# Attention phase: stacked operands filled from SBUF, transpositions placed inside accumulations, and Q of two groups ahead of K

## The chip, the cores and the metric

The program runs on one core of one Trainium2 chip. Its time is device microseconds (us) of one execution; the number compared is the median over repeated executions. The kernel before takes 1622.26 us (median of 3 runs, 1620.95 to 1627.36). All five engines of the core are used: PE (TensorE, matmul), DVE (VectorE), ACT (ScalarE), POOL (GpSimd) and SP (SyncE, which here only issues DMAs).

## The reference

Eight independent batches of 512 tokens with 512 features go through two layers. Only the first attention is touched by the change; in short:

```python
h   = layernorm(x)                                   # (8, 512, 512)
q, k, v = h @ W_Q + b_Q, ctx @ W_K + b_K, ctx @ W_V + b_V   # 16 heads of 32
attn = softmax(q @ k.T / sqrt(32)) @ v               # per head
x = x + tanh(g_xattn[0]) * (attn @ W_O + b_O)
x = x + tanh(g_ffn[0])   * bitlinear_ffn(layernorm(x))       # 8-bit activations, ternary weights
x = x + tanh(g_xattn[1]) * softmax(layernorm(x) @ ctx.T) @ ctx
x = x + tanh(g_ffn[1])   * mxfp4_linear(layernorm(x))
```

## The kernel before

**Phases.** `attention_phase` computes the first attention of all eight batches (about the first 864 us of the span); `ffn_and_final_phases` does everything after it. The change is in the first phase only.

**Precision by splitting.** Every f32 operand of a projection or a score is held as a high part and a low part (HI = rounded copy, LO = the rest), and a product is three passes, HI·HI, LO·HI and HI·LO. For scores the three passes are stacked along the contraction: a head has 32 features, so `stack[:, g, Q]` holds HI, LO, HI on partitions 0 to 31, 32 to 63, 64 to 95, and `stack[:, g, K]` holds HI, HI, LO. One matmul with 96 rows then gives a score tile. Row 96 holds ones on the K side and minus the row maximum on the Q side (`mrow`), so that the 97-row matmul gives the score less its maximum.

**Groups and slots.** Four heads (J = 4) make a group g of 128 features, four groups make a batch. For each group there are 16 steps, called slots here: one `max` matmul (96 rows; DVE reduces its row maximum, L843), and one `score` matmul (97 rows; ACT takes the exponential, L724). Twelve of the 16 exponentials are added up on POOL (L938). After the slots come the matmuls with V (`pv`, L627), and the column sums (`den`, L646), for which all of POOL's sums must be done. PE also does, between slots, the work for the batch ahead: transpositions of x and ctx tiles (`t`, L550: t0 to t3 of x, t4 to t7 of ctx), the Q and K projections (`qk`, L566: 12 matmuls each, in four pieces of 3), and the V projection of the batch itself (`v`, L580: 4 tiles of 12 matmuls).

**What sets the order.** `Clock` is a table of due times in ticks; a group has 160, a slot 8. Each engine runs all steps in the order of their times (plus an offset per engine), written out without a loop. `ahead(n)` puts a step at slot n of a count that starts with group 1 of the batch before, so that the work ahead is spread over groups 1, 2, 3 of one batch; V stands in group 0. Times only set the order; the engines run as fast as their semaphores let them.

**Two PSUM banks.** t, qk and v share banks `work0` and `work1`. `Turns` hands them out in turn, and PE waits until the bank's last user was read by both ACT and DVE.

**From a projection to the stack.** ACT writes the HI part of a projection with its bias to `part[:, side, HI]`, DVE the LO part (L691, L830). `part` has one place for Q and one for K. SP then sends both parts to DRAM (`spill`, 512 KB, L456), and when they have landed issues three loads of 256 KB (`fill`, L464), each of which takes four heads from four blocks of 32 rows to 32 partitions of `stack`. A place of `part` is free again for ACT when the spill has landed. The first `max` of group g stands 19 slots before its first `score` and waits for both fills of its group. SP issues every DMA of the phase, `mrow` among them (L470), in the order of the table, and while it waits for one, those behind it wait too.

Of the kernel before, what the change touches and what calls it, by code (L numbers as in the profile page):

```python
# [151 lines left out]
class Turns:  # L152
# [4 lines left out]
    def __init__(self, banks, users, batches, read_out):  # L157
        self.banks, self.users, self.batches, self.read_out = banks, users, batches, read_out
        self.turn = {key: n for n, (_, key) in enumerate(users)}
        assert len(users) % len(banks) == 0  # L160

    def bank(self, *key):
        return self.banks[self.turn[key] % len(self.banks)]

    def wait_free(self, engine, it, *key):
        n, back = self.turn[key] - len(self.banks), 0
        while back <= 3:
            while n < 0:
                n, back = n + len(self.users), back + 1
            shift, who = self.users[n]  # L170

            if not isinstance(it, int) or 0 <= it - back + shift < self.batches:
                self.read_out(engine, it, shift - back, who)
                return
            n -= len(self.banks)


def attention_phase(nc, NB, keep0, keep1, x, ctx_in, w_q, b_q, w_k, b_k, w_v, b_v, spill, attn_t, ctx_t, ffn_w, w_o, b_o, weight, delta_w,
# [54 lines left out]
    with ExitStack() as ctx:  # L233
# [12 lines left out]
        ct = wo  # L246
        stage = sb("stage", [P, STAGE, D], F32)
# [21 lines left out]
        brow = mrow[0:3 * G, 0, :].bitcast(F32)  # L269
# [14 lines left out]
        wv_lo, bias_turned, bias_done, ln_nmean = sem("wv_lo"), sem("bias_turned"), sem("bias_done"), sem("ln_nmean")  # L284
# [22 lines left out]
        spilled = [sem("spilled_q"), sem("spilled_k")]  # L307
# [18 lines left out]
        tx_at, tc_at = (0, 1.5, 3, 4.5), (10.8, 12.3, 13.8, 15.3)  # L326
        qk_at = {(0, Q): 6, (0, K): 16.8, (1, Q): 21.4, (1, K): 26, (2, Q): 30.6, (2, K): 35.2, (3, Q): 39.8, (3, K): 44.4}
        fill_at = {(0, Q): 17, (0, K): 25, (1, Q): 32, (1, K): 37, (2, Q): 41, (2, K): 46, (3, Q): 52, (3, K): 56}
        STORE_CT = (50, 57.5)
        ck = Clock(G * PERIOD, NB)  # L330
        for i in range(T):
# [6 lines left out]
            for c in range(C):  # L338
                ck.add(round(7.4 * (i * C + c)), 2, "v", i, c)
        for n, slot_n in enumerate(STORE_CT):  # L340
            ck.add(ahead(slot_n), 9, "ctstore", n)
        for g in range(G):
            base = g * PERIOD
            for side in (Q, K):
                for c in range(C):
                    ck.add(ahead(qk_at[g, side] + 1.15 * c), 3, "qk", g, side, c)
                ck.add(ahead(qk_at[g, side] + 1.15 * (C - 1)) + at["spill"], 9, "spill", g, side)
# [41 lines left out]
        def read_out(pe, it, shift, who):  # L389
# [5 lines left out]
            elif kind == "qk":  # L395
                wait_count(pe, qk_hi, it, shift, 2 * G, 2 * n + who[2] + 1)
                wait_count(pe, qk_lo, it, shift, 2 * G, 2 * n + who[2] + 1)
# [9 lines left out]
        turns = Turns(work, users, NB, read_out)  # L407
# [4 lines left out]
        with nc.Block() as block:  # L412
            @block.sync
            def _(sp):
# [13 lines left out]
                def window(it, shift, name, args):  # L428
# [23 lines left out]
                    elif name == "spill":  # L452
                        g, side = args
                        sync_wait(sp, held, qk_lo, it, shift, 2 * G, 2 * g + side + 1)
                        sync_wait(sp, held, stacked[g][side], it, shift, 1, 0, 48)
                        sp.dma_start(spill[g, side].rearrange("h p s -> p h s"), part[:, side].bitcast(F32))\  # L456
                            .then_inc(spilled[side], 16)
                    elif name == "fill":
                        g, side = args
                        sync_wait(sp, held, spilled[side], it, shift, G, g + 1, 16)  # L460

                        sync_wait(sp, held, s_full, it, shift, G * T * J, (g - G + 1) * T * J)
                        for n, h in enumerate((HI, LO, HI) if side == Q else (HI, HI, LO)):
# [3 lines left out]
                    elif name == "mrow":  # L467
                        g, = args
                        sync_wait(sp, held, mt_done, it, shift, G, g + 1)
                        sp.dma_start(stack[96:97, g, Q].bitcast(F32), mrow[:, g % 2, :].bitcast(F32))\  # L470
                            .then_inc(mrow_put[g % 2], 16)
# [40 lines left out]
                    elif name == "boload" and b == NB - 1:  # L512
                        sp.wait_ge(spilled[Q], 16 * G * NB)
                        sp.wait_ge(spilled[K], 16 * G * NB)
# [10 lines left out]
            def _(pe):  # L525
# [3 lines left out]
                def turn_biases():  # L529
                    pe.wait_ge(bias_loaded, 48)  # L530
                    nc.tensor.transpose(den[:, 0:3 * G], brow[:], ident[0:3 * G, 0:3 * G]).then_inc(bias_turned, 1)
# [7 lines left out]
                def window(it, shift, name, args):  # L539
# [13 lines left out]
                    elif name == "qk":  # L553
                        g, side, c = args
                        if c == 0:
                            if isinstance(it, int) and it + shift == 0 and g == 0:
                                pe.wait_ge(w_hi, side + 1)
                                pe.wait_ge(w_lo, side + 1)
                                pe.wait_ge(bias_done, 1)
# [91 lines left out]
            def _(act):  # L651
                def split_weight(n):
                    act.wait_ge(w_loaded[n], 16)
                    nc.scalar.activation(w["qkv"[n]][:, :, HI, :], probs[:, n], ACT.Copy).then_inc(w_hi, 1)
# [10 lines left out]
                def put_biases():  # L665
                    act.wait_ge(bias_turned, 1)
                    nc.scalar.activation(bias[:].rearrange("p n g -> p (n g)"), den[:, 0:3 * G], ACT.Copy).then_inc(bias_done, 1)
                    act.wait_ge(bias_done, 1)

                def window(it, shift, name, args):  # L670
# [16 lines left out]
                    elif name == "qk" and args[2] == C - 1:  # L687
                        g, side, _ = args
                        wait_count(act, qk_full, it, shift, 2 * G, 2 * g + side + 1)
                        wait_count(act, spilled[side], it, shift, G, g, 16)  # L690
# [5 lines left out]
                    elif name == "norm":  # L696
# [5 lines left out]
                        if isinstance(it, int) and it + shift == 0 and i == T - 2:  # L702
                            split_weight(0)
                    elif name == "v" and args[1] == C - 1:
# [4 lines left out]
                    elif name == "mt":  # L709
# [3 lines left out]
                        nc.scalar.activation(mrow[:, g % 2, :], den[0:J * T, 0:P], ACT.Copy).then_inc(mt_done, 1)  # L713
                    elif name == "score":
# [1098 lines left out]
```

## Time and profile before

| | us |
|---|---|
| median of 3 runs | 1622.26 |
| the profiled execution | 1623.71 |
| its span, first to last instruction | 1621.9 |
| PE busy (share of the span) | 1477.0 (91%) |
| DVE busy | 1226.8 (76%) |
| ACT busy | 875.9 (54%) |
| POOL busy | 890.9 (55%) |
| mean granted TensorE clock, of full speed | 0.958 |

The span is 1.8 us shorter than the execution's own time. Busy shares are means over stages with different limits, so they say little of one stage. Of its DMA the page gives 265.32 MB in all, with 64 spills (512 KB each, median 3.5 us from issue to landing) and 192 loads into the stack (256 KB each, 6.8 us).

### The profile page before, as it was taken

How to read it: one execution, taken by the hardware profiler on the slowest of the kernel's cores; microseconds unless marked ns; L12 is line 12 of the kernel's file. 1: busy time of each engine (PE TensorE's matmuls, PEld its weight loads, DVE VectorE, ACT ScalarE, POOL GpSimd, SP SyncE). 2: the span in 40 equal slices, each digit the busy share in tenths (PEclk: the TensorE clock that was granted, in tenths of full speed). 3: DMA queues.
4: the chain of work that ended last, by engine and by line, in shares of the span. 5: the costliest groups of instructions: out<-in, count | busy, mean ns of one | idle time of the engine just before them, and what ended most of it. 6: DMA issues, size and time to landing. Idle time of an engine off the chain costs nothing. (4 is left out here: it accounts for less than half of the span.)

```text
span 1621.9 us, 24716 instructions
## 1 busy us (share of the span) xinstructions
PE 1477.0 (91%) x6993; PEld 937.9 (58%) x6993; DVE 1226.8 (76%) x2135; ACT 875.9 (54%) x1433; POOL 890.9 (55%) x1148
## 2 busy tenths in 40 slices
PE   5699999999999889899784999999999968999997
PEld 3466666556565566655532455555555447887885
DVE  4867677777868677677662788888888848999986
ACT  4156666666565556555453555555555535555552
POOL 3166676585675757656462343343333316777775
PEclk9899999999999989999878999999999989999998
DMA  6757849485694865937941344444444653556522
GB/s 201 227 163 211 258 150 273 143 249 161 185 277 128 229 190 176 289 108 226 251 115 55 95 114 109 109 116 107 107 107 109 190 146 120 167 165 203 166 86 62
DMA packets 252172, 265.32 MB, mean 164 GB/s; under 512 B 139932, under 2 KB 162984, under 8 KB 247720
## 3 DMA queue, kind: packets, MB, share of 16 engines
q1 hardware_dynamic: 252072, 264.14, 57.4%
q8 instruction: 44, 0.72, 0.2%
q14 instruction: 56, 0.46, 0.1%
HBM read 149.50 MB, written 82.87 MB: 143 GB/s over the span
## 5 line engine op out<-in xcount | busy, mean ns | idle before, releaser
L724 ACT ACTIVATE a_probs<-a_sc 128x512 f32<-128x512 f32 x512 | 300.5, 595 | 288.5 <-PE a_sc L608 284.7
L843 DVE TENSOR_REDUCE a_negmax<-a_mx 128x1 f32<-128x512 f32 x512 | 339.0, 675 | 108.1 <-PE a_mx L591 107.3
L938 POOL TENSOR_TENSOR a_acc<-a_acc,a_probs 128x512 f32<-128x512 f32 x248 | 311.6, 1285 | 11.1 <-ACT a_probs L724 9.7
L938 POOL TENSOR_TENSOR a_acc<-a_probs 128x512 f32<-128x512 f32 x124 | 156.9, 1285 | 247.9 <-ACT a_probs L724 247.0
L591 PE MATMUL a_mx<-a_stack 96*128 96x512 f32 x512 | 231.0, 451 | 40.3 <-DVE a_negmax L843 22.3
L1089 PE MATMUL bank<-wcode,b_xq 128*128 128x512 bf16 x1024 | 229.3, 383 | 11.1 <-DMA b_xq<-b_xcode 11.1
L608 PE MATMUL a_sc<-a_stack 97*128 97x512 f32 x512 | 217.7, 427 | 21.0 <-DMA a_stack<-a_mrow 19.5
L1089 PEld LDWEIGHTS bank<-wcode,b_xq 128*128 128x128 bf16 x1024 | 100.5, 98 | 135.0 <-DMA b_xq<-b_xcode 12.5
L854 DVE RECIPROCAL a_attn<-a_den 128x128 f32<-128x128 f32 x128 | 120.8, 947 | 71.1 <-PE a_den L646 58.6
L591 PEld LDWEIGHTS a_mx<-a_stack 96*128 96x128 f32 x512 | 103.1, 201 | 114.4 <-DVE a_negmax L843 55.0
L1127 ACT ACTIVATE b_sig<-bank,b_tok 128x512 f32<-128x512 f32 x128 | 87.4, 683 | 94.0 <-PE bank L1089 91.9
L608 PEld LDWEIGHTS a_sc<-a_stack 97*128 97x128 f32 x512 | 104.0, 203 | 49.5 <-DMA a_stack<-a_mrow 18.4
L566 PE MATMUL a_work<-a_xt,k_wbuf 128*128 128x512 f32 x384 | 121.5, 431 | 12.0 <-DVE a_xt L818 12.0
L1181 DVE TENSOR_TENSOR b_hid<-b_sig,bank 128x512 f32<-128x512 f32 x128 | 87.4, 685 | 50.8 <-ACT b_sig L1127 50.8
L1131 ACT ACTIVATE b_hid<-b_hid,b_htok 128x2048 f32<-128x2048 f32 x32 | 64.1, 2003 | 102.9 <-DVE b_htok L1200 102.9
L627 PE MATMUL a_pvb<-a_probs,a_v 128*32 128x512 f32 x1024 | 118.9, 603 | 0.7 <-ACT a_probs L724 0.7
L1096 PE MATMUL bank<-wcode,b_hq 128*128 128x512 bf16 x512 | 116.1, 380 | 0.0
L566 PE MATMUL a_work<-k_wo,k_wbuf 128*128 128x512 f32 x384 | 114.5, 410 | 1.5 <-DVE k_wo L818 1.5
L1078 PE MATMUL bank<-k_wo,b_apart 128*128 128x512 f32 x384 | 101.8, 415 | 14.7 <-POOL b_apart L1232 13.8
L580 PE MATMUL a_work<-k_wbuf,k_wo 128*128 128x512 f32 x384 | 113.9, 409 | 0.0
L1503 PE MATMUL bank<-c_ct,c_xt 128*128 128x512 f32 x384 | 99.0, 408 | 11.0 <-DVE c_xt L1601 8.7
L1238 POOL TENSOR_TENSOR b_nmean<-b_mv,k_minus 128x1 f32<-128x1 f32 x32 | 6.1, 189 | 172.0 <-DVE b_mv L1153 172.0
(165 smaller groups left out, 2637.0 us busy)
## 6 DMA issues: line engine op xcount, KB each, us to landing
a_stack<-spill SPq DMA_DIRECT2D x192, 256.0 KB, 6.8
spill<-k_part SPq DMA_DIRECT2D x64, 512.0 KB, 3.5
ctx_t<-k_wo SPq DMA_DIRECT2D x16, 1024.0 KB, 9.8
c_ct<-ctx_t SPq DMA_DIRECT2D x8, 2048.0 KB, 7.9
a_stage<-in_x_dram SPq DMA_DIRECT2D x32, 256.0 KB, 5.1
a_stage<-in_ctx_dram SPq DMA_DIRECT2D x32, 256.0 KB, 3.1
a_wsum<-in_L_ffn_w_gate_dram SPq DMA_DIRECT2D x8, 1024.0 KB, 6.1
attn_t<-a_attn SPq DMA_DIRECT2D x32, 256.0 KB, 4.6
```

Of the source, the lines that this page charges most:

```text
L566: last = nc.tensor.matmul(turns.bank("qk", g, side)[:], w["qk"[side]][:, c, a, g * P:(g + 1) * P], src[:, c, m, :], start=c == 0 and n == ...
L580: last = nc.tensor.matmul(turns.bank("v", i)[:], ct[:, c, a, i * P:(i + 1) * P], w["v"][:, c, m, :], start=c == 0 and n == 0, stop=c == C ...
L591: nc.tensor.matmul(mx[i % 2][:], stack[0:96, g, Q, j, t * P:(t + 1) * P], stack[0:96, g, K, j, :], start=True, stop=True).then_inc(mx_full, 1)
L608: nc.tensor.matmul(sc[i % 2][:], stack[0:97, g, K, j, k * P:(k + 1) * P], stack[0:97, g, Q, j, :], start=True, stop=True).then_inc(s_full, 1)
L627: last = nc.tensor.matmul(pvb[DH * j:DH * (j + 1), :], v[:, k, h * DH:(h + 1) * DH], probs[:, k, j, :], start=k == 0, stop=k == T - 1)
L724: nc.scalar.activation(probs[:, k, j, :], sc[i % 2][:], ACT.Exp, scale=SCALE).then_inc(exp_done, 1)
L843: nc.vector.tensor_reduce(negmax[:, g % 2, j, t:t + 1], mx[i % 2][:], axis=AX.X, op=ALU.max, negate=True).then_inc(mx_done, 1)
L854: nc.vector.reciprocal(attn[:, g % 2, q * P:(q + 1) * P], den[:, q * P:(q + 1) * P]).then_inc(recip_done, 1)
L938: nc.gpsimd.tensor_tensor(acc[:, j], probs[:, 0, j] if k == 1 else acc[:, j], probs[:, k, j], ALU.add)\
L1078: last = nc.tensor.matmul(bank_o[:], apart[:, t % 2, a, c, :], wo[:, c, m, :], start=c == 0 and n == 0, stop=c == C - 1 and n == 2)
L1089: last = nc.tensor.matmul(bank[:], xq[:, t % 2, c, :], gu_code[:, side * M + m, :, c, :], start=c == 0, stop=c == C - 1)
L1096: last = nc.tensor.matmul(bank_d[:], hq[:, t % 2, r, :], wcode[:, 2 * M:3 * M, r, :], start=r == 0, stop=r == R - 1)
```

## The change

1. The spill to DRAM is gone. The columns of W_Q, W_K and their biases are permuted within a group when the weights are split (`permuted`, and a second transposed bias row `bpart`), so that partition 4r + j of a projection is feature r of head j. The three fills then read `part` in SBUF, in row order, and write the stack. A place of `part` is free for ACT when the three fills that read it have landed.
2. `mrow` is issued by ACT's DMA queue, not by SP's.
3. The table: transpositions of x move from group 1 into group 0 among the V accumulations; those of ctx move forward into the Q accumulations of groups 0 and 1; Q of group 1 comes before K of group 0. `BANK` names each user's bank, so that a transposition inside an accumulation has the other bank.

```diff
+        def permuted(n, h):
+            to = w["qkv"[n]][:, :, h, :]
+            src = probs[:, n].rearrange("p a b -> p (a b)").rearrange("p (c e) -> p c e", c=C)
+            if n == 2:
+                return to, src
+            return (to.rearrange("p c (g r j) -> p c g r j", g=G, j=J), src.rearrange("p c (g j r) -> p c g r j", g=G, j=J))
...
-        tx_at, tc_at = (0, 1.5, 3, 4.5), (10.8, 12.3, 13.8, 15.3)
-        qk_at = {(0, Q): 6, (0, K): 16.8, (1, Q): 21.4, (1, K): 26, ...
+        tx_at, tc_at = (-14.5, -10.7, -7.2, -3.7), (2, 7, 9.7, 11.2)
+        v_at = [3.6 * i + 0.9 * c for i in range(T) for c in range(C)]
+        ORDER = ((0, Q), (1, Q), (0, K), (1, K), (2, Q), (2, K), (3, Q), (3, K))
+        RANK = {key: n for n, key in enumerate(ORDER)}
...
-                    elif name == "spill":
-                        g, side = args
-                        sync_wait(sp, held, qk_lo, it, shift, 2 * G, 2 * g + side + 1)
-                        sync_wait(sp, held, stacked[g][side], it, shift, 1, 0, 48)
-                        sp.dma_start(spill[g, side].rearrange("h p s -> p h s"), part[:, side].bitcast(F32))\
-                            .then_inc(spilled[side], 16)
                     elif name == "fill":
                         g, side = args
-                        sync_wait(sp, held, spilled[side], it, shift, G, g + 1, 16)
+                        sync_wait(sp, held, qk_lo, it, shift, 2 * G, RANK[g, side] + 1)
                         sync_wait(sp, held, s_full, it, shift, G * T * J, (g - G + 1) * T * J)
                         for n, h in enumerate((HI, LO, HI) if side == Q else (HI, HI, LO)):
-                            sp.dma_start(stack[DH * n:DH * (n + 1), g, side].bitcast(F32),
-                                         spill[g, side, h].rearrange("(j r) s -> r j s", j=J))\
+                            sp.dma_start(stack[DH * n:DH * (n + 1), g, side].bitcast(F32), part[:, side, h].bitcast(F32))\
                                 .then_inc(stacked[g][side], 16)
...
+                    elif name == "mrow":
+                        g, = args
+                        wait_count(act, mt_done, it, shift, G, g + 1)
+                        nc.scalar.dma_start(stack[96:97, g, Q].bitcast(F32), mrow[:, g % 2, :].bitcast(F32))\
+                            .then_inc(mrow_put[g % 2], 16)
...
                         g, side, _ = args
-                        wait_count(act, qk_full, it, shift, 2 * G, 2 * g + side + 1)
-                        wait_count(act, spilled[side], it, shift, G, g, 16)
+                        wait_count(act, qk_full, it, shift, 2 * G, RANK[g, side] + 1)
+                        wait_count(act, stacked[(g - 1) % G][side], it, shift, 1, 1 if g else 0, 48)
...
-                        if it + shift == 0 and (g, side) == (1, Q):
+                        if it + shift == 0 and (g, side) == (1, K):
                             dve.wait_ge(exp2_done, 2)
                             dve.wait_ge(gated, 1)
                             for n in range(3, 6):
                                 quantise(n)
```

On PE, at the start of group 1 of batch 0, right after the column sums of group 0, the rows before are these (`a_work0` and `a_work1` are the two shared banks; `a_work<-k_ident` is a transposition, `a_work<-a_xt` a piece of a Q projection):

```order
L646 MATMUL a_den<-a_acc,a_ones 32x512 x4
L550 MATMUL a_work0<-k1_ident,a_stage 128x128 x4
L591 MATMUL a_mx1<-a_stack 128x512
L608 MATMUL a_sc0<-a_stack 128x512
L591 MATMUL a_mx0<-a_stack 128x512
L608 MATMUL a_sc1<-a_stack 128x512
L550 MATMUL a_work1<-k1_ident,a_stage 128x128 x4
L591 MATMUL a_mx1<-a_stack 128x512
L608 MATMUL a_sc0<-a_stack 128x512
L550 MATMUL a_work0<-k1_ident,a_stage 128x128 x4
```

and at the same place now:

```order
L651 MATMUL a_den<-a_acc,a_ones 32x512 x4
L571 MATMUL a_work0<-a_xt,k0_wbuf 128x512 x3
L596 MATMUL a_mx1<-a_stack 128x512
L613 MATMUL a_sc0<-a_stack 128x512
L596 MATMUL a_mx0<-a_stack 128x512
L613 MATMUL a_sc1<-a_stack 128x512
L571 MATMUL a_work0<-a_xt,k0_wbuf 128x512 x3
L555 MATMUL a_work1<-k1_ident,a_stage 128x128 x4
L596 MATMUL a_mx1<-a_stack 128x512
L613 MATMUL a_sc0<-a_stack 128x512
```

The transpositions of x have left this place, Q of group 0 starts at once in bank 0, and the first transposition of ctx stands inside it, in bank 1.

On ACT, in the middle of group 1, the second projection of Q (`k_part`, group 1) is now read here, behind a wait for the fills of group 0 (`a_stacked0_q`), ahead of the exponentials and of two ctx transpositions:

```order
L741 ACTIVATE a_probs<-a_sc 128x512 [waits a_acc_done,a_pv_full,a_s_full]
L699 ACTIVATE k_part<-a_work,a_bias 128x512 [waits a_stacked0_q,a_qk_full]
L746 ACTIVATE a_attn<-a_attn,a_bias 128x512 [waits a_attn_done]
L741 ACTIVATE a_probs<-a_sc 128x512 [waits a_acc_done,a_s_full]
L690 ACTIVATE k_wo<-a_work 128x4x128 [waits a_t_full]
L741 ACTIVATE a_probs<-a_sc 128x512 [waits a_acc_done,a_s_full] x2
L690 ACTIVATE k_wo<-a_work 128x4x128 [waits a_t_full]
```

Before, the nearest such read, K of group 0 in the early slots of group 2, waited for a spill and had only exponentials and the output's bias behind it:

```order
L691 ACTIVATE k_part<-a_work,a_bias 128x512 [waits a_spilled_k,a_qk_full]
L724 ACTIVATE a_probs<-a_sc 128x512 [waits a_s_full] x3
L724 ACTIVATE a_probs<-a_sc 128x512 [waits a_acc_done,a_pv_full,a_s_full]
L729 ACTIVATE a_attn<-a_attn,a_bias 128x512 [waits a_attn_done]
L691 ACTIVATE k_part<-a_work,a_bias 128x512 [waits a_spilled_q,a_qk_full]
```

So the wait of ACT is for another transfer, and what queues behind it is more.

## Rows read from the trace of the kernel before

A row of windows gives the stretch (us from the span's start) and its length, then busy us (and the count of instructions) of PE, PE's weight loads, DVE, ACT and POOL, the granted clock as a share of full speed, the busy share of the DMA engines, and GB/s. In a timeline, the brackets hold the idle time ahead of an instruction and what ended it.

**Rows 1.** Windows: a batch, four later batches, groups 1 and 2 of the last.
```profile
292.57:388.01 95.44, 90.56 (x470) 59.37 (x470) 70.23 (x108) 61.06 (x112) 64.40 (x64) 0.98 0.70 209
388.01:795.18 407.17, 374.61 (x1881) 244.22 (x1881) 305.49 (x468) 235.77 (x404) 261.13 (x240) 0.95 0.69 199
795.18:825.43 30.25, 20.28 (x74) 10.29 (x74) 18.84 (x24) 11.99 (x19) 14.82 (x12) 0.66 1.01 230
825.43:847.70 22.27, 19.32 (x71) 8.54 (x71) 12.95 (x19) 9.95 (x18) 14.80 (x12) 0.69 0.29 63
```

**Rows 2.** Windows: one batch by groups, in the order 1, 2, 3, 0.
```profile
196.96:221.83 24.87, 21.62 (x119) 13.51 (x118) 19.54 (x30) 16.19 (x31) 14.94 (x12) 0.93 0.37 120
221.83:245.63 23.80, 22.67 (x117) 14.81 (x116) 17.78 (x28) 13.85 (x25) 17.16 (x20) 1.00 0.73 215
245.63:269.10 23.47, 22.92 (x118) 14.82 (x116) 18.42 (x29) 15.71 (x28) 17.01 (x20) 1.00 0.99 287
269.10:292.57 23.47, 23.47 (x123) 16.29 (x123) 14.58 (x21) 15.37 (x28) 15.30 (x13) 1.00 0.76 224
```

**Rows 3.** Timeline of PE: start, us, then the instruction; group 0 and its end.
```profile
97.33 3.64 PE L627 MATMUL a_pvb<-a_probs,a_v 128*32 128x512 f32 x32
100.79 1.04 PE L646 MATMUL a_den<-a_acc,a_ones 128*32 128x512 f32 x8
101.76 0.66 PE L550 MATMUL a_work<-k_ident,a_stage 128*128 128x128 f32 x4
102.17 0.48 PE L591 MATMUL a_mx<-a_stack 96*128 96x512 f32 x1
...
270.30 0.86 PE L580 MATMUL a_work<-k_wbuf,k_wo 128*128 128x512 f32 x3
271.47 0.87 PE L580 MATMUL a_work<-k_wbuf,k_wo 128*128 128x512 f32 x3
```

**Rows 4.** Timeline of POOL: the twelve sums of one group.
```profile
275.86 5.05 POOL L938 TENSOR_TENSOR a_acc<-a_probs 128x512 f32<-128x512 f32 x4 [6.58 <-ACT a_probs L724]
280.87 10.20 POOL L938 TENSOR_TENSOR a_acc<-a_acc,a_probs 128x512 f32<-128x512 f32 x8
```

**Rows 5.** Waits of PE over the span: us in total, times, longest.
```profile
PE a_sc L608 <- DMA a_stack<-a_mrow: 19.5, 6, 8.5
PE a_mx L591 <- issue: 12.7, 11, 2.0
```

**Rows 6.** Timeline of PE in group 1, and the window behind its stall.
```profile
205.13 1.41 PE L566 MATMUL a_work<-a_xt,k_wbuf 128*128 128x512 f32 x3 [1.64 <-DVE a_xt L818]
...
205.00:208.40 3.40, 3.27 (x8) 2.62 (x9) 2.69 (x4) 0.71 (x2) 1.08 (x2) 0.56 0.05 17
```

**Rows 7.** The fills issued at 231.79 us, then those at 220.8 us.
```profile
231.79 1.25 SPq L464 DMA_DIRECT2D a_stack<-spill  x3
DMA to landing us min/median/max: 3.2/4.1/4.6
...
DMA to landing us min/median/max: 6.8/7.4/7.8
```

**Rows 8.** Timeline of SP and PE in the last batch, group 1.
```profile
795.32 5.41 SPq L507 DMA_TRANSPOSE wcode<-code_t  x1
800.86 0.56 SPq L470 DMA_DIRECT2D a_stack<-a_mrow  x1
...
804.14 0.79 PE L608 MATMUL a_sc<-a_stack 97*128 97x512 f32 x1 [8.53 <-DMA a_stack<-a_mrow]
```

**Rows 9.** Timeline of PE and DVE at the start.
```profile
45.16 0.77 PE L591 MATMUL a_mx<-a_stack 96*128 96x512 f32 x1 [4.98 <-DMA a_stack<-spill]
76.59 0.77 PE L608 MATMUL a_sc<-a_stack 97*128 97x512 f32 x1 [3.29 <-DMA a_stack<-a_mrow]
...
39.82 2.79 DVE L776 SCALAR_TENSOR_TENSOR a_attn<-a_attn 128x64 f32<-128x64 f32 x1
45.96 0.69 DVE L843 TENSOR_REDUCE a_negmax<-a_mx 128x1 f32<-128x512 f32 x1 [0.43 <-PE a_mx L591]
```

More of the change, by code:

```diff
@@ L152, with __init__ @@
 class Turns:
-    def __init__(self, banks, users, batches, read_out):
+    def __init__(self, banks, users, batches, read_out, chosen=None):
         self.banks, self.users, self.batches, self.read_out = banks, users, batches, read_out
         self.turn = {key: n for n, (_, key) in enumerate(users)}
-        assert len(users) % len(banks) == 0
+        self.chosen = chosen or {key: n % len(banks) for n, (_, key) in enumerate(users)}
+        assert chosen or len(users) % len(banks) == 0
     def bank(self, *key):
-        return self.banks[self.turn[key] % len(self.banks)]
+        return self.banks[self.chosen[key]]
     def wait_free(self, engine, it, *key):
-        n, back = self.turn[key] - len(self.banks), 0
+        n, back = self.turn[key] - 1, 0
         while back <= 3:
@@ L170, in wait_free, with attention_phase @@
             shift, who = self.users[n]
-            if not isinstance(it, int) or 0 <= it - back + shift < self.batches:
+            if self.chosen[who] == self.chosen[key] and (not isinstance(it, int) or 0 <= it - back + shift < self.batches):
                 self.read_out(engine, it, shift - back, who)
                 return
-            n -= len(self.banks)
-def attention_phase(nc, NB, keep0, keep1, x, ctx_in, w_q, b_q, w_k, b_k, w_v, b_v, spill, attn_t, ctx_t, ffn_w, w_o, b_o, weight, delta_w,
+            n -= 1
+def attention_phase(nc, NB, keep0, keep1, x, ctx_in, w_q, b_q, w_k, b_k, w_v, b_v, attn_t, ctx_t, ffn_w, w_o, b_o, weight, delta_w,
                     delta_act, g_xattn, g_ffn, w1_code, code_t):
@@ L268, in attention_phase @@
         e2, ie, cw = (attn[:, 0, n * C * NBL:(n + 1) * C * NBL] for n in range(3))
-        brow = mrow[0:3 * G, 0, :].bitcast(F32)
+        brow, bpart = (mrow[0:3 * G, n, :].bitcast(F32) for n in range(2))
         wsrc = [m.rearrange("(o p) i -> p o i", p=P) for m in ffn_w]
@@ L345, in attention_phase @@
                 for c in range(C):
-                    ck.add(ahead(qk_at[g, side] + 1.15 * c), 3, "qk", g, side, c)
-                ck.add(ahead(qk_at[g, side] + 1.15 * (C - 1)) + at["spill"], 9, "spill", g, side)
+                    ck.add(ahead(qk_at[g, side][c]), 3, "qk", g, side, c)
                 ck.add(ahead(fill_at[g, side]), 9, "fill", g, side)
@@ L406, in attention_phase @@
                 users.append((shift, (name, *args[:-1])))
-        turns = Turns(work, users, NB, read_out)
+        turns = Turns(work, users, NB, read_out, BANK)
         def stage_wait(engine, it, shift, i):
@@ L653, in split_weight @@
                     act.wait_ge(w_loaded[n], 16)
-                    nc.scalar.activation(w["qkv"[n]][:, :, HI, :], probs[:, n], ACT.Copy).then_inc(w_hi, 1)
+                    to, at_n = permuted(n, HI)
+                    nc.scalar.activation(to, at_n, ACT.Copy).then_inc(w_hi, 1)
                 def small_tables():
@@ L666, in put_biases @@
                     act.wait_ge(bias_turned, 1)
-                    nc.scalar.activation(bias[:].rearrange("p n g -> p (n g)"), den[:, 0:3 * G], ACT.Copy).then_inc(bias_done, 1)
-                    act.wait_ge(bias_done, 1)
+                    flat = bias[:].rearrange("p n g -> p (n g)")
+                    nc.scalar.activation(flat[:, 0:2 * G], den[:, 3 * G:5 * G], ACT.Copy).then_inc(bias_done, 1)
+                    nc.scalar.activation(flat[:, 2 * G:3 * G], den[:, 2 * G:3 * G], ACT.Copy).then_inc(bias_done, 1)
+                    act.wait_ge(bias_done, 2)
                 def window(it, shift, name, args):
@@ L703, in window @@
                             split_weight(0)
+                        if it + shift == 0 and i == T - 1:
+                            act.wait_ge(bias_loaded, 48)
+                            nc.scalar.activation(bpart[:].rearrange("n (r j) -> n r j", j=J), brow[:].rearrange("n (j r) -> n r j", j=J),
+                                                 ACT.Copy).then_inc(bias_put, 1)
                     elif name == "v" and args[1] == C - 1:
@@ L1770, in build_program @@
     NB, S, D = x.shape
-    spill = nc.dram_tensor("spill", [4, 2, 2, P, S], F32, kind="Internal").ap()
     attn_t = nc.dram_tensor("attn_t", [NB, D // P, P, S], F32, kind="Internal").ap()
```

40 lines of the change are left out of this document (20 added, 20 removed).

## The prediction, made before the changed kernel ran

> **What bounds the kernel now.** I read the windows by batch first, then by group, then the waits of PE, and only then single rows. A batch of the early stretch takes 95.4 us, three of them alike, at a clock of 0.98 [rows 1]. Cut into its groups it takes 24.87, 23.80, 23.47 and 23.47 us (groups 1, 2, 3, 0) [rows 2]. Group 0 is PE's: it is busy for all of it. A slot with a piece of a projection is five matmuls in 1.17 us (271.47 less 270.30), so a matmul is 0.234 us, a piece 0.70 and a bare slot 0.47; the V matmuls take 3.46 us, the column sums 0.97 and a transposed tile 0.41 [rows 3]. Sixteen slots with sixteen pieces are 18.7 us, with the tail of 4.43 it makes 23.2, and 23.47 stands there.
>
> The other groups are not PE's alone. Group 1 holds eight transposed tiles and only four pieces, PE busy 21.62 of 24.87 us: it stalls on a transposed tile that DVE has not split (1.64 us), and in the 3.4 us behind that stall the clock is 0.56, that is mostly at 1.2 GHz [rows 6]. Behind PE stands POOL. Its twelve sums take 15.2 us, one every 1.26 us [rows 4]. The first waits for the exponential of slot 4, the last must be done ahead of the column sums. With bare slots the last batch shows what this chain gives: group 2 takes 22.27 us with PE far from full work [rows 1]. I take 22 us as the least for a group, whatever PE does.
>
> From 388 to 795 us four batches take 407.17 us, 25.6 more than four early ones [rows 1]. There the ternary codes are made at the ends of groups, and SP, which also issues the mrow transfer, is held up by waits for them. PE waits 19.5 us for mrow in six places [rows 5]: 3.29 at the start [rows 9], 8.53 in the last batch [rows 8], so 7.7 in the four between.
>
> **The spill removed.** SP loses 64 issues and PE loses no work. The trace has no transfer of this size from SBUF to SBUF, so its cost is bounded: three fills from DRAM, with little else in flight, land 3.2 to 4.6 us after their issues, those behind a 1 MB load 6.8 to 7.8 [rows 7]. I take the quiet ones, 5.4 us from the first issue to the last landing (0.85 for the issues ahead, 4.6), since the source's traffic falls away, and keep 4 and 8.6 as ends. What it buys in the steady part is small: in group 2 PE stands before its first max matmul for fills that come late, part of the 12.7 us put down to issue [rows 5], one to two us a batch.
>
> **The new wait of ACT.** `part` is free only when the fills have landed, not the spill. In group 1, counted from the end of the column sums, Q of group 0 is complete at 5.1 us (four slots, four pieces, one tile). DVE splits it behind four reciprocals and five maxima, at about 7.3; the last fill lands at 7.3 + 5.4 = 12.7. Q of group 1 is complete at 10.7. So ACT stands about 1.5 us, and behind it the output's bias, exponentials and two transposed tiles. K of group 0 needs the last of these tiles, split by DVE: I get 17 us for its start, where PE alone would be there at 13.4. From there three pieces and three slots (3.5 us) and 4.43 make 25. With fills that land at once the chain of the last tile alone still gives 23.8. I take 24.9: group 1 stays as it is. In group 2 the same wait stands between K of group 0 and K of group 1, 1 to 2.5 us, most of it under POOL's chain.
>
> **A steady batch.** Group 0 takes four tiles more and is PE's: 23.47 + 4 × 0.41 = 25.1, +1.6. Group 1: 0 (bounds: -2, POOL's chain, which starts after five slots with four pieces, 22.8; +2). Group 2 has 11 pieces where it had 14, so POOL decides: 21.9 by its chain, and about 1 for ACT's wait and a halved clock behind it: 22.9, -0.9. Group 3 has 10 pieces: 22.3, -1.2. Sum -0.5 a batch, seven batches, of which four are counted below: -1.5 here.
>
> **mrow on ACT.** The issue costs ACT 0.56 us or so (SP's in rows 8), beside POOL's chain: nothing. In the four late batches the 7.7 us of waits go. Three of the four are followed by a window at half clock, worth 1.7 each; the clock over this stretch is 0.95 against 0.98, which would allow up to 12 us [rows 1]. I take 5 for it, and 0.5 a batch as above: -14.7. The code work itself stays, about 13 us. In the last batch group 1 took 30.25 us; without the 8.53 it falls onto POOL's 22.3: -7.9. What is late next there is the exponentials' chain, as in rows 1.
>
> Here a rule speaks against the change. In the trace SP is busy 5.41 us with one transposing DMA, issues mrow only then, and it lands 3.3 us later [rows 8]. The Trainium skill (DMA: Bandwidth & Descriptors, Issuing engines are not separate DMA queues) has it that transfers from any engine run on the same 16 DMA engines and interleave, and that a second issuer saves only the sequencer's time. By that the 5.41 us of issue are saved and the landing is not, and it may be longer, with the transposition's packets still ahead. The wait of 8.53 then becomes 3.1 or more, the gain 5.4 or less, and the sum -16.9. No row here shows an mrow that was issued early beside a transposition, so I leave the sum as the rows of PE give it.
>
> **The start.** Q of group 1 and two ctx tiles come before K of group 0, and the second Q waits on ACT for the fills of the first, with weight loads in flight. K of group 0 begins about 5.5 us later than it did. Then K of group 1 waits for K of group 0's fills, and DVE's scaling of the last layer's weight, 6.1 us from 39.82 to the first max at 45.96 [rows 9], stands behind that split. I get the first max on DVE about 9 us later. Against this two splits are done already (-1.4), and mrow's 3.29 us go: +4.7 (bounds 0 and +9).
>
> **Sum.** -1.5 - 14.7 - 7.9 + 4.7 = -19.4 on 1623.7 of the profiled execution. After the attention nothing changes. As the profiled execution stands 1.4 above the median of 1622.3, I put the forecast at 1603 us. Its own range is 1594 to 1612.
>
> **Rival A: the fills land early.** SBUF to SBUF is quicker (4 us from first issue), ACT does not stand, the clock stays up. Then the groups fall to the floors: 25.1, 22.8, 21.9, 22.1 = 91.9, -3.5 for each of seven batches, -24.5, with mrow's 12.7 and 7.9 and the start at +2: -43, 1579. For it: DMA traffic falls by 64 × 512 KB twice over. Against it: the chain of the last ctx tile, which doesn't ask for the fills.
>
> **Rival B, slower: part becomes the bound.** If fills land as those at 220.8 us did, 3.2 us later than I take, ACT stands that much longer in group 1 and, with POOL's slack of 1.9 gone over, 1.3 longer in group 2: 4.5 a batch, 31.5 in seven: 1635. It decides where three fills take over 6 us while a 1 MB weight load is on its way. For it: in most groups such a load is issued just ahead of them. Against: that load has mostly landed when the first of the two is due. It would pass the old time when the fills take 5 us more than the 5.4 taken, or 3 with a worse start.
>
> **Rival C: nearly nothing.** The rule on issuers holds fully (mrow's waits fall only by the issue, 6 us less gained at the end and 4 in between), and PE's idle time ahead of the column sums halves its clock at the starts of groups: 1603 + 10 + 3 = 1616.
>
> **Chances.** Forecast 0.50, A 0.20, C 0.16, B 0.14. I count 0.5%, 8 us, as what can be told from no change, so from 1614 to 1630 is no change. Faster: nearly all of the forecast's and A's, 0.67. Same: C and the edge of the forecast, 0.19. Slower: B, 0.14. For 8 in 10 the range is 1582 to 1632, with half of A below it and most of B above.
>
> **What would show it.** In the windows by group: group 0 at 25, groups 2 and 3 near 22.5, group 1 still near 25 with PE waiting for the split of a ctx tile. In ACT's waits: `k_part` waiting for the stack's DMA, 1 to 2 us twice a batch; none, and it is A; 4 or more, and it is B. The row of mrow in PE's waits falls from 19.5 to under 5 us; if not, it is C. The first score matmul at about 81 us, not 76.6. POOL's first sum of a group should follow the column sums by 6 to 8 us and its last end just ahead of the next ones, with PE idle before them; if PE isn't, POOL isn't the floor I take it for. The forecast is wrong at its root if group 0 stays at 23.5 or group 1 falls under 23.

## The result and the profile after

The changed kernel takes 1693.8 us (median of 4, 1693.04 to 1697.18), the kernel before on the same chip 1621.9 (1620.95 to 1627.36): ratio 1.0438, 95% interval 1.0414 to 1.0461. I had forecast 1603 and given the slower side 0.14. The wait that rival B named did it, at over two and a half times B's price (B had 31.5 us for seven batches; against experiment 2 they take 82 us more).

The windows of one steady batch, in the order of [rows 2] (groups 1, 2, 3, 0), then groups 1 and 2 of the last batch (against [rows 1]):

```profile
228.57:259.52 30.95, 25.73 (x124) 17.16 (x123) 17.96 (x27) 15.18 (x28) 15.04 (x12) 0.83 0.33 74
259.52:290.17 30.65, 22.63 (x108) 14.58 (x107) 17.68 (x28) 13.79 (x25) 16.37 (x18) 0.89 0.78 134
290.17:312.32 22.15, 20.00 (x105) 12.53 (x104) 17.50 (x28) 14.82 (x27) 16.74 (x18) 1.00 0.74 163
312.32:337.93 25.61, 25.53 (x139) 17.69 (x138) 16.87 (x25) 17.75 (x32) 16.32 (x17) 1.00 0.88 230
870.54:894.13 23.59, 19.63 (x74) 9.45 (x74) 19.45 (x26) 12.00 (x19) 14.84 (x12) 0.71 1.09 244
894.13:916.18 22.05, 19.28 (x71) 8.26 (x71) 12.95 (x19) 10.07 (x18) 14.82 (x12) 0.69 0.49 104
```

Group 0 is PE's at 25.6 (25.1 was worked out), and group 3 falls to 22.15, POOL's floor. The last batch's group 1 gives back 6.7 of its 30.25. But groups 1 and 2 take 6.1 and 6.9 us more than in [rows 2]. The waits of ACT and PE over the span (us in total, times, longest) name the place:

```profile
ACT k_part L699 <- DMA a_stack<-k_part: 87.1, 18, 8.4
...
PE a_sc L613 <- ACT a_probs L741: 68.2, 20, 7.7
```

PE waited 19.5 us for mrow in [rows 5]; now it is 1.6. Instead it waits 68.2 for exponentials, which stand on ACT behind an eviction into `part` that waits for the fills. Timelines of SP, ACT and PE, with the landings of the three fills at 235.93 and of the three from 262.7 on:

```profile
235.93 1.85 SPq L473 DMA_DIRECT2D a_stack<-k_part  x3
DMA to landing us min/median/max: 4.2/5.7/6.8
...
244.04 0.69 ACT L699 ACTIVATE k_part<-a_work,a_bias 128x512 fp32r<-128x512 f32 x1 [4.67 <-DMA a_stack<-k_part]
...
245.87 0.80 PE L613 MATMUL a_sc<-a_stack 97*128 97x512 f32 x1 [4.57 <-ACT a_probs L741]
...
257.49 0.38 SPq L490 DMA_DIRECT2D a_wsum<-in_L_ffn_w_up_dram  x1
258.06 6.46 SPq L473 DMA_DIRECT2D a_stack<-k_part  x6
DMA to landing us min/median/max: 9.9/10.9/11.7
...
275.71 0.69 ACT L699 ACTIVATE k_part<-a_work,a_bias 128x512 fp32r<-128x512 f32 x1 [8.35 <-DMA a_stack<-k_part]
...
276.94 0.80 PE L613 MATMUL a_sc<-a_stack 97*128 97x512 f32 x1 [7.66 <-ACT a_probs L741]
```

Read it from below. At 275.71 ACT evicts K of group 1, 8.35 us late, because K of group 0's fills have just landed. The last of these was issued at 263.9 and took 11.7, behind a 1 MB load and three fills of Q. The windows around this wait show what it does to PE and its clock:

```profile
265.00:270.00 5.00, 4.19 (x17) 2.76 (x15) 3.52 (x6) 1.54 (x3) 3.78 (x3) 1.00 1.09 147
270.00:275.00 5.00, 0.00 (x0) 0.00 (x0) 0.00 (x0) 0.00 (x0) 0.00 (x0) 0.94 0.78 106
275.00:280.00 5.00, 3.06 (x7) 2.46 (x8) 3.06 (x5) 2.96 (x6) 3.04 (x3) 0.50 0.33 64
```

From 270 to 275 PE has no work at all, and behind that it runs at half clock (1.2 GHz). In group 1 the same happens milder: 8.0 us from the first issue to the last landing where I had taken 5.4. There the loss has two parts: against experiment 2, whose order of work is the same, PE's idle time is 5.2 us instead of 1.3, and its busy time 25.7 instead of 22.5, with a granted clock of 0.83 instead of 1.00.

The ledger, from the ends of the column sums: the first stands at 119.51 (101.83 before), +17.7; the seven batches to the last one's group 0, 751.0 against 693.4, +57.7; groups 1 and 2 of the last, -6.9. That is 68.5 of the 73.5 us between the two spans (1695.4 and 1621.9); the other 5.0 lie in the last group and behind the attention, where I had put nothing and looked for no cause.

### The profile page after: what moved, and what is told of

Read it like the earlier page. It is cut to its first block and busy times, and to the rows that moved or that the text cites. A ratio compares the mean times of both kernels' runs of the same rounds, so it can differ in the third digit from the quotient of the medians.

```text
span 1695.4 us, 24511 instructions
## 1 busy us (share of the span) xinstructions
PE 1505.3 (89%) x6994; PEld 959.1 (57%) x6994; DVE 1228.1 (72%) x2135; ACT 881.4 (52%) x1435; POOL 891.7 (53%) x1148
## 5 line engine op out<-in xcount | busy, mean ns | idle before, releaser
L860 DVE TENSOR_REDUCE a_negmax<-a_mx 128x1 f32<-128x512 f32 x512 | 334.8, 672 | 75.6 <-PE a_mx L596 72.6
L613 PE MATMUL a_sc<-a_stack 97*128 97x512 f32 x512 | 226.6, 445 | 69.9 <-ACT a_probs L741 68.2
L596 PE MATMUL a_mx<-a_stack 96*128 96x512 f32 x512 | 235.1, 460 | 25.4 <-DVE a_negmax L860 20.3
L1106 PE MATMUL bank<-wcode,b_xq 128*128 128x512 bf16 x1024 | 229.8, 383 | 10.7 <-DMA b_xq<-b_xcode 10.7
L613 PEld LDWEIGHTS a_sc<-a_stack 97*128 97x128 f32 x512 | 108.5, 213 | 101.9 <-ACT a_probs L741 79.7
L596 PEld LDWEIGHTS a_mx<-a_stack 96*128 96x128 f32 x512 | 106.6, 208 | 95.2 <-DVE a_negmax L860 52.0
L571 PE MATMUL a_work<-k_wo,k_wbuf 128*128 128x512 f32 x384 | 126.1, 445 | 6.9 <-DVE k_wo L835 6.1
L847 DVE SCALAR_TENSOR_TENSOR k_part<-a_work,a_bias,k_part 128x512 fp32r<-128x512 f32 x64 | 47.7, 745 | 96.3 <-ACT k_part L699 96.3
L1095 PE MATMUL bank<-k_wo,b_apart 128*128 128x512 f32 x384 | 102.4, 416 | 14.8 <-POOL b_apart L1249 13.8
```

The costliest lines, as they stand in the source:

```text
L571: last = nc.tensor.matmul(turns.bank("qk", g, side)[:], w["qk"[side]][:, c, a, g * P:(g + 1) * P], src[:, c, m, :], start=c == 0 and n == ...
L596: nc.tensor.matmul(mx[i % 2][:], stack[0:96, g, Q, j, t * P:(t + 1) * P], stack[0:96, g, K, j, :], start=True, stop=True).then_inc(mx_full, 1)
L613: nc.tensor.matmul(sc[i % 2][:], stack[0:97, g, K, j, k * P:(k + 1) * P], stack[0:97, g, Q, j, :], start=True, stop=True).then_inc(s_full, 1)
L860: nc.vector.tensor_reduce(negmax[:, g % 2, j, t:t + 1], mx[i % 2][:], axis=AX.X, op=ALU.max, negate=True).then_inc(mx_done, 1)
L1095: last = nc.tensor.matmul(bank_o[:], apart[:, t % 2, a, c, :], wo[:, c, m, :], start=c == 0 and n == 0, stop=c == C - 1 and n == 2)
L1106: last = nc.tensor.matmul(bank[:], xq[:, t % 2, c, :], gu_code[:, side * M + m, :, c, :], start=c == 0, stop=c == C - 1)
```

## The experiments

Each was run beside the kernel before on the same chip; the ratio is to it. In steady batches the comparison is by the ends of the column sums.

**1. mrow alone.** The transfer is issued by ACT, all else as before.

```
-  sp.dma_start(stack[96:97, g, Q]..., mrow[:, g % 2, :]...)
+  nc.scalar.dma_start(stack[96:97, g, Q]..., mrow[:, g % 2, :]...)
```

> The kernel before, with the mrow transfer alone issued by ACT instead of SP; order, banks and spill as before. My theory is that this part of the change did what was predicted and the loss is elsewhere: PE's waits for mrow fall from 19.5 us to under 4, and the time falls by 12 to 20 us, to 1602 to 1610. The rival says that an issue among ACT's exponentials costs as much as the waits did (32 issues, beside the scores): then mrow's row falls too, but ACT's exponentials come late by as much, and the time stays within 5 us of 1622.

1602.9 us, ratio 0.9873 (0.9818 to 0.9928). PE's waits for mrow fall to 4.6 us in three places, a little over the 4 expected. This part of the change brings about 20 us by itself; the prediction had 23.9 for it (12.7 in the late batches, 7.9 in the last, 3.3 at the start), and the ends of the column sums give 12.8, 6.5 and 2.9.

**2. The new order with the spill kept.**

```
   (changed kernel)
+  sp.dma_start(spill[g, side]..., part[:, side]...)            # as before
-  sp.dma_start(stack[...], part[:, side, h]...)
+  sp.dma_start(stack[...], spill[g, side, h].rearrange("(j r) s -> r j s", j=J))
-  ACT waits for stacked[(g - 1) % G][side]
+  ACT waits for spilled[side]
```

> The changed kernel with its new order, banks and mrow on ACT, but with the way through DRAM put back: part is spilled in 512 KB, is free as soon as the spill has landed, and the fills read the spill. Theory 1, the direct fills are the whole loss: groups 1 and 2 take 25 and 23 us instead of 30.9 and 30.5, ACT waits for part less than 10 us in all (87.1 with direct fills), and the time is 1595 to 1615. Rival 1, the order itself (Q of two groups ahead of K, the last ctx tiles just ahead of K of group 0) is slow whatever fills: group 1 stays at 28 us or more and the time above 1660. Rival 2, the clock: 0.93 with few waits, and a time between, 1630 to 1660.

1600.5 us, ratio 0.9845 (0.9786 to 0.9904), 93 us less than the changed kernel. ACT waits for `part` 9.8 us in all, not 87.1. (The columns of the weights stand unpermuted again, as the fill through DRAM sorts the rows.) Windows of one batch, groups 1, 2, 3, 0:

```profile
204.67:228.46 23.79, 22.52 (x124) 15.01 (x123) 17.69 (x27) 14.95 (x28) 15.00 (x12) 1.00 0.44 136
228.46:250.60 22.14, 21.17 (x108) 12.94 (x107) 16.01 (x24) 13.81 (x25) 15.04 (x12) 1.00 0.85 245
250.60:276.06 25.46, 21.62 (x105) 13.53 (x104) 19.09 (x32) 14.93 (x27) 18.06 (x24) 0.93 0.74 229
276.06:301.67 25.61, 25.55 (x139) 17.69 (x138) 16.87 (x25) 17.78 (x32) 16.30 (x17) 1.00 0.71 220
```

The order is not at fault: groups 1 and 2 take 23.8 and 22.1, the "fills that land at once" and POOL floors of the prediction, within 0.3. The clock as a cause by itself falls with it: with fills that don't hold ACT, PE stays busy and the clock is 1.00 in both groups. Where the next group has 25.46, a load of the x tiles stands behind a fill's wait (experiments 8 and 9).

**3. Direct fills in the old order, 6. the same with mrow on ACT.** Order, banks and tiles as before, the fills from `part` 2.5 slots after its last piece.

```
-  spill; fill from spill;      ACT waits for spilled[side]
+  fill from part;              ACT waits for stacked[(g - 1) % G][side]
```

> The kernel before with its old order, banks and mrow on SP, and only the direct fills: no spill, the fills read part 2.5 slots after its last piece, ACT waits until they have landed. In this order two pieces of the same side stand 9 slots apart (10.8 us) instead of 5. Theory 1a, only fills of 8 us together with two parts 5 slots apart make the loss: ACT waits for part under 25 us in all, and the time stays within 12 us of 1622. Theory 1b, fills of 8 us hurt in any order, since the first max matmuls wait for them: PE waits for the stack's DMA by 2 us or more in each group, and the time is over 1650. The rival, that direct fills are harmless and the order does it, has the time at 1622 or below with ACT's waits for part under 5 us.

> Old order with direct fills as in the third experiment (1662 us), and mrow issued by ACT. There PE waited 41 us for mrow, which stood behind fills of 6.6 us on the same DMA engines. If the wait came from SP's order of issues, mrow's row falls under 5 us and the time to 1620 or below. If it came from the DMA engines, busy with the fills whoever issues, mrow's row stays at 15 us or more and the time at 1635 to 1655.

Experiment 3: 1662.2 us (1.0231, 1.0173 to 1.0289). Experiment 6: 1649.5 (1.0169, 1.0137 to 1.0201). So direct fills lose in the old order too, 47 us against experiment 1, but half of the 93. My 1a, "within 12 us of 1622", failed; its ACT waits held. 1b had the time (over 1650) but not the reason: a first max matmul waited for the fills once, 5.2 us. The waits:

```profile
ACT k_part L699 <- DMA a_stack<-k_part: 20.7, 8, 6.7
...
PE a_sc L613 <- DMA a_stack<-a_mrow: 41.0, 15, 5.8
...
PE a_sc L608 <- DMA a_stack<-a_mrow: 21.2, 13, 6.2
```

(ACT and PE of 3, PE of 6.) What PE waits for here is mrow, which lands 6.6 us after an issue at 233.82, behind three fills issued at 230.91, and after 2.0 us at 209.98 with none ahead. Moving its issue off SP halves the wait and no more: the median landing is still 6.2 us (5.8 in 3). This wait is not all of the 47 us: it is 21.2 us where experiment 1 has 4.6. DVE also waits 29.1 us for x tiles, against 3.4, and the first column sums end 10.9 us later; the rest I did not divide up. The median in the changed kernel, where fills and mrow rarely meet, is 1.8.

**4 and 7. The transfers alone.**

> Not the attention at all: only transfers, each set waited for before the next, twice over, and the output is not computed. Sets of three transfers of 256 KB: DRAM to 32 partitions each (rows of 2 KB), SBUF 128 partitions to 32, DRAM in rows of 8 KB to 32, SBUF 128 to 128, DRAM to 128, SBUF 32 to 32 on the same and on other partitions; and single ones. The theory that moving between partitions of SBUF is slow in itself: three fills from SBUF take about 8 us from first issue to last landing and from DRAM 5.4, with nothing else in flight. If the 32 partitions at the target make it, the set of 128 to 128 is quicker than 128 to 32, and DRAM to 32 is slower than DRAM to 128. The rival, that it was the loads beside them: all sets within 1 us of each other, at about 5.4.

> Only transfers again, the output is not computed. The same three fills as twelve transfers of 64 KB from 32 partitions to 32; three transfers within their own 32 partitions; 128 partitions to 64; a spill waited for and then the three fills; both ways behind a 1 MB load; and mrow's transfer alone, behind three direct fills and behind three fills from DRAM. Theory: from 128 partitions to 32 is the slow case, to 64 lies between (3 us), spill and fills take 8 us together as the direct fills do; behind a load the direct fills land 2 to 3 us later than from DRAM, and mrow behind direct fills at 7 us or more, behind fills from DRAM at 4 to 5, alone at 2. Rival: the rate follows the number of bytes only, and mrow lands alike behind both.

Timeline of SP in 4; each set of three waits for the one before, so the step from start to start is a set's time:

```profile
14.73 1.25 SPq L35 DMA_DIRECT2D dst<-rows  x3
19.82 2.00 SPq L38 DMA_DIRECT2D dst<-src  x3
27.98 1.85 SPq L41 DMA_DIRECT2D dst<-src  x3
36.00 1.26 SPq L44 DMA_DIRECT2D dst<-rows  x3
...
46.64 1.82 SPq L50 DMA_DIRECT2D dst<-src  x3
50.33 1.76 SPq L53 DMA_DIRECT2D dst<-src  x3
```

From DRAM to 32 partitions each 5.1 us, from 128 partitions of SBUF to 32 8.1, but from 128 to the same 128 only 3.7. The windows while each flows, in that order:

```profile
11.50:14.00 2.50, 0.00 (x0) 1.00 1.00 220
...
22.50:26.50 4.00, 0.00 (x0) 1.00 1.05 122
...
49.00:50.20 1.20, 0.00 (x0) 1.00 0.76 285
```

All 16 DMA engines are busy in the second (share 1.05), and move 122 GB/s; in the first they are as busy (1.00) and move 220. So it is not SBUF as a source by itself; the slow sets are those that gather rows of 128 partitions into few. No set moved rows crosswise among 128 partitions, so whether the crossing or the few partitions make it is open. Sets from DRAM in rows of 8 KB took 5.1 to 5.5, and 32 partitions to 32 in rows of 8 KB 5.4 to 5.7. The Trainium skill (SBUF — State Buffer, Door 1: The DMA port swizzle) has it that partitions 0 to 31 and 0 to 63 reach the same half of SBUF's ports; one transfer of 256 KB from 128 partitions took 4.0 us to 32 and 3.9 to 64, which agrees and refutes my expectation that 64 lie between. That rule is of one side of a transfer: the set from DRAM writes the same 32 partitions and takes 5.1 us, so it does not tell the two apart.

In 7 a spill and its three fills took 8.0 to 8.2 us together, as much as the direct fills, but the spill is over after 2.8. Behind a 1 MB load the direct fills ended at 11.3 to 11.8 and fills from DRAM, without a spill, at 8.4 to 8.6. With the spill between load and fills the whole took 12.4, longer than the direct way, but the spill had landed after 7.1. Landings of mrow's transfer alone, behind three direct fills (7 expected), behind three from DRAM:

```profile
DMA to landing us min/median/max: 1.8/1.8/1.8
...
DMA to landing us min/median/max: 6.3/6.3/6.3
...
DMA to landing us min/median/max: 4.2/4.2/4.2
```

The fills as twelve transfers of 64 KB took 8.9 us, 7.6 of it issue.

**5. The hold without the slow transfers.** Experiment 2, through DRAM, but ACT waits for the fills.

```
-  wait_count(act, spilled[side], it, shift, G, g, 16)
+  wait_count(act, stacked[(g - 1) % G][side], it, shift, 1, 1 if g else 0, 48)
```

> New order, banks, mrow on ACT, spill and fills through DRAM as in the second experiment (1600 us), but ACT may write part again only when the fills have landed, not the spill: the changed kernel's wait with the other kernel's transfers. Spill and fills one after the other took 2.8 and 5.1 us by themselves, the direct fills 8.1, so part is held as long. Theory 1, what costs is that part is held for 8 us where the next Q comes 5 slots later: the loss returns without any transfer inside SBUF, groups 1 and 2 take 30 us, ACT waits for part 60 us or more, time 1670 to 1700. The rival, what costs is what the transfers inside SBUF take from the 16 DMA engines (other loads and mrow come late): then the time stays under 1630.

1681.0 us, ratio 1.0346 (1.0316 to 1.0376). One line changed against experiment 2, 80.5 us lost. Waits of ACT, and the windows of groups 1 and 2:

```profile
ACT k_part L707 <- DMA a_stack<-spill: 85.3, 17, 8.9
...
225.73:256.58 30.85, 25.56 (x124) 16.97 (x123) 17.96 (x27) 15.19 (x28) 15.03 (x12) 0.83 0.34 108
256.58:286.19 29.61, 23.34 (x107) 15.05 (x107) 17.68 (x28) 13.90 (x25) 16.70 (x19) 0.88 0.69 194
```

Group 1 is the changed kernel's to 0.1 us, group 2 is 1.0 shorter, and the clocks are 0.83 and 0.88 (0.83 and 0.89 there). So about 80 of the 93 us are the hold of `part`, and about 13 come on top with the slower transfers (by the ratios to the kernel before 81 and 15, the first uncertain by some 10 us, the second by some 6). The ends of the column sums say where these lie: of 14.7 us between the two profiled spans 2.9 at the start, 6.8 in the seven batches, 1.5 in groups 1 and 2 of the last, 3.5 behind.

**8 to 10. Versions meant to beat both.** 8 keeps the spill, has mrow on ACT and the groups in the old order (K of group 0 ahead of Q of group 1), the x tiles inside V's accumulations and the ctx tiles around Q of group 0. 9 is experiment 2, 10 is 8, each with SP's loads of the x tiles moved ahead:

```
-  load=(-860, -850, -740, -730)
+  load=(-932, -931, -850, -849)     # 9;  10: (-935, -934, -850, -849)
-  ORDER = ((0, Q), (1, Q), (0, K), (1, K), (2, Q), ...)
+  ORDER = ((0, Q), (0, K), (1, Q), (1, K), (2, Q), ...)      # 8, 10
```

> A version that may beat both: spill kept, mrow on ACT, x tiles inside V's accumulations and ctx tiles spread around Q of group 0 on the other bank, but the groups in the old order, K of group 0 ahead of Q of group 1. By the groups: group 0 25.6 us as in the second experiment, groups 1 to 3 at 23 to 23.5, so a batch as there (94.5), and the start as in the first (99 us to the end of the first column sums, not 108.5): 1590 to 1597. The rival: without Q of group 1 between the ctx tiles and K of group 0, PE stands there for the last split by DVE, group 1 stays at 25 and the time at 1600 or above.

> The second experiment's kernel (new order, spill kept, mrow on ACT; 1600 us), with SP's loads of the x tiles moved ahead of the spill and fills of K of group 1. There, at the start, POOL and ACT stood 13.2 us for the LayerNorm of an x tile that SP loads only behind a fill's wait, and the first column sums ended at 108.5 us against 99.0 with the old order. If SP's queue makes the late start, the first sums end at 99 to 103 and the time is 1590 to 1596; if the order of Q and K makes it, they stay at 108 and the time within 3 us of 1600.

> The mixed version (K of group 0 ahead of Q of group 1, tiles inside the V or Q accumulations, spill kept; 1626 us), with the same loads moved ahead. There DVE stood 5.3 to 10.7 us for an x tile that SP loaded behind a fill's wait, and group 3 took 27 us. If SP's queue is the cause, group 3 takes 23 us, the start ends at 99 to 102, and the time is 1585 to 1597. If not, group 3 stays at 26 us or more and the time above 1615.

8: 1626.3 us (1.0027, 1.0011 to 1.0043), a miss, for a reason that neither side had. DVE, which takes its work in order, stood for an x tile whose load waited on SP behind a fill's wait for its spill:

```profile
60.06 0.69 DVE L830 BATCH_NORM_STATS2 a_stats<-a_stage 128x6 f32<-128x512 f32 x1 [10.70 <-DMA a_stage<-in_x_dram]
```

9: 1589.0 (0.9787, 0.9758 to 0.9815). The first column sums end at 106.4, not 99 to 103: the gain of 11 us came from group 3 (22.2 instead of 23 to 25.5), and only 2 of it at the start. 10: 1585.8 (0.9776, 0.9750 to 0.9802), the best; its first sums end at 100.1. Its batch, groups 1, 2, 3, 0:

```profile
193.75:218.43 24.68, 21.46 (x118) 13.57 (x117) 17.88 (x27) 15.05 (x28) 14.99 (x12) 1.00 0.43 135
218.43:240.16 21.73, 21.59 (x111) 13.50 (x110) 17.58 (x28) 13.89 (x25) 15.98 (x16) 1.00 0.82 220
240.16:261.88 21.72, 21.24 (x108) 12.71 (x107) 17.46 (x28) 14.92 (x27) 17.07 (x21) 1.00 0.80 245
261.88:287.47 25.59, 25.50 (x138) 17.68 (x138) 16.87 (x25) 17.75 (x32) 16.29 (x17) 1.00 0.81 260
```

93.7 us a batch against 95.4 [rows 1].

**11 and 12. The hold, and the direct fills, where there is room.** 11 is 10 with the hold of experiment 5, 12 is 10 with the direct fills and their hold (and the fills a little earlier in the table, as there is no spill ahead of them). Two parts of one side stand 10.7 slots or more apart here; in the new order Q of groups 0 and 1 stand 4.9 apart and K 5.9.

> The same as the mixed version with loads ahead, but ACT may write part again only when the fills have landed, as in the fifth experiment, which that wait made 81 us slower. Here two parts of the same side stand 10.8 slots apart instead of 5. Theory: a hold of 8 us costs only where the next part of that side is due sooner; ACT's waits for part fall from 85 us to under 15 and the time is within 12 us of the mixed version without the hold. Rival: the hold costs in any order, as ACT's queue is blocked whenever the fills are late: over 30 us more.

> The mixed version with loads ahead (1585.8 us), but the spill is gone and the fills read part directly, part held until they have landed, as in the changed kernel: its direct fills in an order where two parts of one side stand 10.8 slots apart. The hold alone cost 9 us there. If what is left of the loss in the changed kernel (1694 against 1681 with the hold alone, 13 us) is the slower traffic's price, the time is 1600 to 1612. If direct fills cost more where they keep the DMA engines busy beside the loads (as in the old order, 47 us with mrow on ACT), it is 1620 or more. If for once they are free, 1595 or less.

11: 1595.0 us (0.9820, 0.9785 to 0.9856). The same line that cost 80.5 us costs 9 here. ACT's waits for part are 24.7 us, a miss of my "under 15"; 13.8 of them are two waits at the start. 12: 1615.9 (0.9945, 0.9922 to 0.9968), between my two cases: 21 more than the hold alone. There mrow lands late again, and PE waits 14.0 us for it in eight places.

## Why the prediction was wrong

- **The fills' cost, the step that failed.** I took 5.4 us from first issue to last landing, from fills out of DRAM [rows 7], "since the source's traffic falls away". Quiet it is 8.0, alone 8.1: near my upper end of 8.6, which I had kept for fills behind a load. Behind a load it is 12.9 (262.7 to 275.6), outside my bounds. There was no row for this path, and I chose the friendly end: the page's median for one fill out of DRAM, 6.8 us from issue to landing, stood before me and was left aside. (In the changed kernel it is 6.7.) This term and the price of a wait, below, were both too small. How the loss divides between the two is open, as no run holds `part` for 5.4 us.
- **The new wait of ACT.** Place and mechanism were right: twice a batch, between Q of groups 0 and 1 and between K of groups 0 and 1. Sizes: 1.5 us forecast, 4.67 measured in group 1; 1 to 2.5 forecast, 8.35 measured in group 2, since Q of group 1's fills queue behind the 1 MB load and K of group 0's behind both. I looked at one set of fills at a time.
- **What a wait costs.** I gave ACT's wait of 1.5 us in group 1 about 1.1 us (24.9 instead of 23.8). Experiments 2 and 5, one line apart, show 7.1 us for a wait of 4.74: 4.0 more of idle time on PE, and 3.0 more of busy time, at a clock of 0.83. I had no term for this half clock in group 1. Rival B had 4.5 a batch, and groups 1 and 2 lost 12.8 a batch in all (89.6 us over seven, against experiment 2); it also left the start as forecast. B's fills, 3.2 us later than mine, come to the 8.6 us that is near the 8.0 measured: its mechanism was right, and for group 1 nearly its duration, but not its price.
- **B's condition** (three fills over 6 us while a 1 MB load is on its way) was met in group 2, at 12.9; in group 1 they took 8.0 with no load on its way. No run has fills of about 6 us, so the threshold itself is not shown.
- **The steady batch** without the hold: 25.1, 24.9, 22.9 and 22.3 forecast; in the changed kernel group 0 is 25.6 and group 3 22.15; in experiment 2 groups 1 and 2 are 23.8 and 22.1. POOL's floor of 22 is nearly right: the least group of a steady batch is 21.7 (experiment 10); group 2 of the last batch fell to 21.1 there.
- **mrow on ACT** (12.7 of the -14.7, then -7.9, beside 3.3 at the start) was right: experiment 1 gives 20 to 22 us in all; in the changed kernel the last batch's group 1 gave back 6.7. The rule that spoke against it (the Trainium skill, DMA: Bandwidth & Descriptors, Issuing engines are not separate DMA queues) was half right: the mrow issued at 865.98 beside a transposing DMA landed after 5.2 us instead of 1.8, but PE waited only 0.23 for it, since ACT issues it 5 us ahead of its use.
- **The start**, +4.7 forecast: +17.7. In experiment 2 it is +6.7 and in experiment 5 +14.7, so of the other 11 about 8 are the hold and 3 the slower transfers. In the changed kernel ACT waits for fills twice there, 7.24 and 6.47 us.
- The forecast of 1603 is near what experiment 2 gives (1600.5), but in part by luck. By the ends of the column sums its seven batches gain 24.4 us where the forecast had 16.2 for them, and this is set off by the start (+6.7 for +4.7), the last batch (-6.4 for -7.9) and 4.5 us behind, where it had nothing.

## What to carry to other kernels

A round trip through DRAM is not only a detour: it frees its source when the first half has landed. Before it is cut out, work out how long the source is held until the last direct transfer lands, and put that beside the time until the buffer's next writer. Here a hold of 8 us and more cost 80 us where that writer came 5 slots later, and 9 where it came 10.7 later. Where the transfer has no like in the trace, measure it by itself, in its own shape of partitions. And ask of each wait on an in-order queue (SP's for a spill, ACT's for a part) what unrelated work stands behind it: moving the four loads of x tiles ahead of such waits gave 40 us in experiment 10 over 8.

## What the runs showed of the hardware

- 256 KB from 128 partitions of SBUF to 32 takes 4.0 us alone, to 64 3.9, from DRAM to 32 2.9. Three such move at 122 GB/s with all DMA engines busy; within the same 128 partitions at 285 GB/s.
- Slow transfers make others late: 8 KB lands after 1.8 us alone, 4.2 behind three fills from DRAM, 6.3 behind three direct ones, all issued by SP (experiment 7). Another issuer did not help: in the old order with direct fills the median is 5.8 us from SP (experiment 3) and 6.2 from ACT (experiment 6).
- TensorE's clock after a wait: PE stands from 270 to 275 us, and its granted clock is 0.50 in the next 5 us (1.00 in the 5 us before).
- Not settled: why DRAM to 32 partitions is not slowed like 128 to 32, and through which waits the slower transfers cost their 13 us in the changed kernel (in experiment 12, where they cost 21, 14.0 are waits for mrow).
